# Last mixture-of-experts stage: one chain of gates, largest scores by comparison, experts of two blocks in one word, shared products earlier

## The reference, cut to what matters

```python
xt = layernorm(x).reshape(-1, 128)                       # 4096 tokens
scores = softmax(xt @ gate_w.T)                          # 4096 x 8
_, idx = top_k(scores + gate_bias, 2)
weights = take_along_axis(scores, idx, axis=1)
for e in range(8):
    gate_e = sum(where(idx == e, weights, 0), axis=1)
    h = silu(xt @ w1[e].T) * (xt @ w3[e].T)
    y = y + gate_e[:, None] * (h @ w2[e].T)
z = silu(xt @ sw1.T) * (xt @ sw3.T) @ sw2.T              # shared, 256 wide
x = x + y + z
```

## Time and profile before

| | |
|---|---|
| median of 3 runs | 1217.52 us (1216.44 to 1219.08) |
| the profiled execution, own time | 1217.4 us |
| its span | 1215.6 us |
| busy, share of the span | PE 79%, DVE 69%, ACT 53%, POOL 38% |
| granted clock of TensorE, mean | 0.898 of full |
| routing of the last stage | 980.7 to 1032.8 us |
| scatter | 1032.8 to 1082.7 us |
| expert blocks | 1082.7 to 1204.0 us |

### The profile page before, as it was taken

How to read it: one execution, slowest core, us unless ns; L and a number is a source line. 1 busy time by engine, 2 the same in 40 slices (tenths; PEclk the granted TensorE clock), 3 DMA queues, 4 the chain that set the end, 5 groups by cost and what they waited for, 6 DMA issues and landing times. The chain is left out here.

```text
span 1215.6 us, 21191 instructions
## 1 busy us (share of the span) xinstructions
PE 964.3 (79%) x7160; PEld 640.0 (53%) x7160; DVE 837.4 (69%) x2167; ACT 643.5 (53%) x1132; POOL 462.9 (38%) x448
## 2 busy tenths in 40 slices
PE   5868810578988997899669999998889886939995
PEld 3653310554556674454326666676645573627774
DVE  4586699857885664677679999999578856314332
ACT  3424568855643454565267877775466531114442
POOL 5610000002210003345099999994111230635443
PEclk9898965779999998999859999998899978969998
DMA  7000000064000000000000000000000000223331
GB/s 276 1 1 1 1 0 0 1 196 134 2 2 1 1 1 1 1 1 2 1 0 1 2 0 0 0 0 1 1 1 2 2 1 1 93 86 91 97 82 26
DMA packets 24235, 33.78 MB, mean 28 GB/s; under 512 B 3484, under 2 KB 20389, under 8 KB 23888
## 3 DMA queue, kind: packets, MB, share of 16 engines
q1 hardware_dynamic: 20720, 26.20, 7.1%
q0 software_dynamic: 3424, 6.38, 1.5%
HBM read 18.34 MB, written 15.98 MB: 28 GB/s over the span
## 5 line engine op out<-in xcount | busy, mean ns | idle before, releaser
L785 DVE TENSOR_REDUCE hq<-psum 128x16 f32<-128x1024 f32 x96 | 114.6, 1221 | 82.0 <-PE psum L519 44.2
L1975 POOL TENSOR_TENSOR big<-big 128x512 f32<-128x512 f32 x128 | 128.6, 1044 | 19.8 <-ACT big L1880 19.8
L429 POOL TENSOR_TENSOR big<-big,w_const 128x256 f32<-128x256 f32 x48 | 36.5, 762 | 260.1 <-PE psum L565 228.3
L1903 ACT ACTIVATE psum<-big,tmp 128x512 f32<-128x512 f32 x128 | 84.9, 686 | 18.9 <-DVE big L2072 16.2
L2580 DVE SCALAR_TENSOR_TENSOR big<-psum,big 128x128 f32<-128x128 f32 x118 | 36.1, 348 | 85.5 <-issue 65.7
L2072 DVE SCALAR_TENSOR_TENSOR big<-big,tmp,psum 128x512 f32<-128x512 f32 x128 | 90.5, 744 | 5.5 <-ACT psum L1903 2.5
L675 ACT ACTIVATE big<-psum 128x1024 f32<-128x1024 f32 x64 | 62.0, 1021 | 54.5 <-PE psum L549 54.5
L790 DVE RECIPROCAL big<-psum 128x256 f32<-128x256 f32 x48 | 84.0, 1751 | 6.1 <-PE psum L565 5.9
L2282 POOL DMA_INDIRECT out<-big x59 | 58.0, 982 | 69.5 <-DVE big L2590 36.9
L1985 POOL TENSOR_TENSOR big<-big 128x1024 f32<-128x1024 f32 x32 | 75.3, 2364 | 11.6 <-DVE big L2072 11.6
L1443 PE MATMUL psum<-f_downT,tmp 128*128 128x128 f32 x192 | 24.9, 293 | 68.0 <-DVE tmp L1326 68.0
(11 more groups left out here) (311 smaller groups left out, 2640.3 us busy)
## 6 DMA issues: line engine op xcount, KB each, us to landing
rows<-pad SPq DMA_DIRECT2D x1, 7670.0 KB, 34.1
big<-rows SPq DMA_DIRECT2D x59, 130.0 KB
tmp<-in_pack_f SPq DMA_DIRECT2D x1, 2051.0 KB, 9.7
w_f<-in_pack_f SPq DMA_DIRECT2D x1, 1280.0 KB, 12.5
tmp<-in_pack_once SPq DMA_DIRECT2D x1, 960.0 KB, 7.1
out<-big POOLq DMA_INDIRECT x59
X<-in_x SPq DMA_DIRECT2D x1, 768.0 KB, 5.2
w_a<-in_pack_a SPq DMA_DIRECT2D x3, 256.0 KB, 8.0
```

The lines of the kernel that those rows point to most:

```text
L785: dve.tensor_reduce(nm, psum[:, 1 + 2 * t:3 + 2 * t, :].rearrange("p c (r l k) -> p (c r) l k", r=2, k=SK), AX.X, ALU.max, negate=True).th ...
L1903: act.activation(bank(EX_BANK + h % 2), ssum[t][:, h * 512:(h + 1) * 512], ACT.Exp, bias=shift2[:, t * NH2 + h:t * NH2 + h + 1]).then_inc( ...
L1975: ins = pool.tensor_tensor(ssum[t][:, h * 512:(h + 1) * 512].rearrange("p (i j) -> p i j", i=ROWS2), st[:, 0, h, 0:ROWS2].unsqueeze(2).to_ ...
```

## The change

Parts of it, in the order of the kernel:
- Normalising: groups 1, 2, 7 on ACT, 3, 4, 5 on POOL. ACT takes group 1 before it finishes the second part of the LayerNorm.
- PE does up(0,0) before the turn of group 1 and up(0,1) after that of group 2. All logits go to one bank, and there is one chain of gates over 32 tiles, behind all logits.
- The two largest scores come by comparison: largest value, where it is equal, times 8 - expert, largest of that; the first is pushed down by 3e38 and the same is done again. MAX8 and FIND_INDEX8 go. The pair's number is worked out from the reversed indices, with constants to match.
- For groups 0 to 2 ACT also copies the second factor out of PSUM, and POOL multiplies; up(g, e) for g = 1 to 3 waits for ACT. DVE does groups 3 to 7.
- PE's order is up(1,0), up(1,1), down(0), up(2,0), up(2,1), counts, down(1), firsts, up(3,0), places, up(3,1), down(2), and on. `places` waits for oh3 and makes the table's products first, one instead of two; add(0) follows the gate columns on DVE.
- The table holds, for two blocks, four experts of five bits in one word. PE loads one word in every second turn, before the transpose, and works out each address with a shift and an AND.
- POOL has a drain ahead of the loop over the blocks and one in its middle.

```diff
@@ -2162,13 +2162,12 @@
+        up3 = [f3.take(GN) for _ in range(2)]
...
-        top3 = f3.take(N_TILES * 8).rearrange("p (t e) -> p t e", e=8)
-        ix3 = f3.take(N_TILES * 8).bitcast(U32).rearrange("p (t e) -> p t e", e=8)
-        ixf3 = f3.take(N_TILES * 2).rearrange("p (t e) -> p t e", e=2)
+        which3 = [f3.take(N_TILES) for _ in range(2)]
@@ -2192,8 +2192,14 @@
-        PARTS3 = ((0, EARLY), (EARLY, N_TILES))
-        ON_ACT, ON_POOL, ON_DVE = (1, 3, 7), (2, 4, 5), (0, 6)
+        POOLED = 3
+        SIL3 = 4 * POOLED + 2 * (N_GROUPS - POOLED)
...
+        def sil_count(g, e):
...
+            return 4 * g + 2 * e + 2 if g < POOLED else 2 * POOLED + 2 * g + e + 1
...
+        ON_ACT, ON_POOL, ON_DVE = (1, 2, 7), (3, 4, 5), (0, 6)
         def f3_normed(pe, g):
@@ -2234,12 +2240,9 @@
-            if 4 * g == EARLY:
-                pe.wait_ge(sem("a3", "res"), at("a3", "res") + N_GROUPS + 1)
-            part = int(4 * g >= EARLY)
...
-                c = 4 * g + t - PARTS3[part][0]
-                ins = pe.matmul(bank(5 + part)[:, c * E3:(c + 1) * E3], hT3[g][:, t * P:(t + 1) * P], W["f3_gate"],
+                c = 4 * g + t
+                ins = pe.matmul(bank(5)[:, c * E3:(c + 1) * E3], hT3[g][:, t * P:(t + 1) * P], W["f3_gate"],
@@ -2266,7 +2269,14 @@
-            pool.wait_ge(S("f3_m"), 6)
+            for g in range(POOLED):
+                for e in range(2):
+                    pool.wait_ge(S("f3_sil"), sil_count(g, e))
+                    if g >= 2:
+                        pool.wait_ge(S("f3_y"), g - 1)
+                    pool.tensor_tensor(hid3[2 * (g % 2) + e], sil3[e], up3[e], ALU.mult).then_inc(S("f3_hid"), 1)
...
+            pool.wait_ge(S("f3_m"), 5)
@@ -2275,7 +2285,10 @@
+            pool.drain()
             for j in range(NB3):
+                if j == NB3 // 2:
+                    pool.drain()
@@ -2297,7 +2310,9 @@
         def f3_pe(pe):
             def up(g, e):
...
-                if g:
+                if 0 < g <= POOLED:
+                    pe.wait_ge(S("f3_sil"), sil_count(g - 1, e))
+                elif g:
@@ -2316,20 +2331,21 @@
             def counts():
-                pe.wait_ge(S("f3_m"), 2)
+                pe.wait_ge(S("f3_m"), 1)
...
             def firsts():
-                pe.wait_ge(S("f3_m"), 3)
+                pe.wait_ge(S("f3_m"), 2)
...
             def places():
...
+                pe.matmul(bank(6)[0:1, 448:508], W["f3_lohi"][0:PAIRS3, :], oh3[0:PAIRS3, :], start=True, stop=True)
@@ -2337,40 +2353,55 @@
-                pe.wait_ge(S("f3_m"), 5)
-                for i in range(2):
-                    ins = pe.matmul(bank(5 + i)[0:1, 448:508], W["f3_lohi"][0:PAIRS3, i:i + 1], oh3[0:PAIRS3, :],
-                                    start=True, stop=True)
...
+            up(0, 0)
...
-            for g in range(2, N_GROUPS):
+            f3_turn(pe, 2)
+            pe.wait_ge(sem("a3", "res"), at("a3", "res") + N_GROUPS + 1)
+            up(0, 1)
+            f3_logits(pe, 1)
+            for g in range(3, N_GROUPS):
...
-            up(0, 0)
-            up(0, 1)
...
+            up(1, 1)
...
-            up(1, 1)
+            up(2, 0)
+            up(2, 1)
...
-            up(2, 0)
...
-            up(2, 1)
+            up(3, 0)
...
-            for g in range(3, N_GROUPS):
+            up(3, 1)
+            down(2)
+            for g in range(4, N_GROUPS):
...
-            pe.wait_ge(S("f3_m"), 7)
+            pe.wait_ge(S("f3_m"), 6)
...
-            first = {}
+            words = {}
...
+            def weights_at(j, k):
...
+                field = 2 * (j % 2) + k
+                w = words[j // 2]
+                w = w << 7 - 5 * field if field < 2 else w >> 5 * field - 7
+                return (w & 31 * P).with_bounds(min_val=0, max_val=(E3 - 1) * 3 * P)
...
             for i in range(NB3 + 3):
+                if i < NB3 and i % 2 == 0:
+                    m = i // 2
+                    _, (words[m],) = nc.values_load_multi_w_load_instructions(
+                        tab3[0:1, m:m + 1], engines=[mybir.EngineType.PE], min_val=0, max_val=2 ** 20 - 1,
+                        skip_runtime_bounds_check_because="the table holds experts' offsets alone")
@@ -2379,16 +2410,12 @@
-                    first[j] = [nc.values_load(tab3[0:1, 64 * k + j:64 * k + j + 1], engines=[mybir.EngineType.PE],
-                                               min_val=0, max_val=(E3 - 1) * 3 * P,
-                                               skip_runtime_bounds_check_because="the table holds experts' offsets alone")
-                                for k in range(2)]
...
-                    for k, r in enumerate(first[j]):
+                    for k in range(2):
...
-                                        W["f3_w"][:, ds(r, 2 * P)], start=True, stop=True)
+                                        W["f3_w"][:, ds(weights_at(j, k), 2 * P)], start=True, stop=True)
@@ -2404,33 +2431,30 @@
-                    for k, r in enumerate(first[j]):
+                    for k in range(2):
...
-                                        W["f3_w"][:, ds(r + 2 * P, P)], start=(k == 0), stop=(k == 1))
+                                        W["f3_w"][:, ds(weights_at(j, k) + 2 * P, P)], start=(k == 0), stop=(k == 1))
...
         def f3_act(act):
-            def exps(part):
-                lo, hi = PARTS3[part]
-                act.wait_ge(S("f3_less"), part + 1)
-                act.activation(prob3[:, lo:hi, :], prob3[:, lo:hi, :], ACT.Exp).then_inc(S("f3_ex"), 1)
...
             def silu(g, e):
...
-            f3_norm_act(act, 3)
+                if g < POOLED:
+                    act.wait_ge(S("f3_up"), 4 * g + 2 * e + 2)
+                    act.activation(up3[e], bank(4 + 3 * e), ACT.Copy).then_inc(S("f3_sil"), 1)
...
+            f3_norm_act(act, 2)
+            f3_take(act, 1)
...
-            f3_take(act, 1)
...
-            f3_take(act, 3)
...
-            for g in range(4, N_GROUPS):
+            for g in range(3, N_GROUPS):
...
-            exps(0)
-            exps(1)
+            act.wait_ge(S("f3_less"), 1)
+            act.activation(prob3, prob3, ACT.Exp).then_inc(S("f3_ex"), 1)
@@ -2459,51 +2483,53 @@
-            def gates(part):
...
-                lo, hi = PARTS3[part]
+            def gates():
...
+                lo, hi = 0, N_TILES
...
-                logits = bank(5 + part)[:, 0:n * E3].rearrange("p (t e) -> p t e", e=E3)
-                dve.wait_ge(S("f3_lg"), hi // GT)
+                logits = bank(5)[:, 0:n * E3].rearrange("p (t e) -> p t e", e=E3)
+                dve.wait_ge(S("f3_lg"), N_GROUPS)
...
-                dve.wait_ge(S("f3_ex"), part + 1)
+                dve.wait_ge(S("f3_ex"), 1)
...
-                settle(dve)
-                for t in range(lo, hi):
-                    dve.max(top3[:, t, :], bias3[:, t, :]).then_inc(S("f3_top"), 1)
-                dve.wait_ge(S("f3_top"), hi + lo)
-                for t in range(lo, hi):
-                    dve.max_index(ix3[:, t, :], top3[:, t, :], bias3[:, t, :]).then_inc(S("f3_top"), 1)
-                dve.wait_ge(S("f3_top"), 2 * hi)
-                step(dve.tensor_copy(ixf3[:, sl, :], ix3[:, sl, 0:2]))
-                step(dve.tensor_tensor(lo3[:, sl], ixf3[:, sl, 0], ixf3[:, sl, 1], ALU.min))
-                step(dve.tensor_tensor(hi3[:, sl], ixf3[:, sl, 0], ixf3[:, sl, 1], ALU.max))
-                step(dve.scalar_tensor_tensor(out=pid3[:, sl], in0=lo3[:, sl], scalar=-13.0, in1=lo3[:, sl],
-                                              op0=ALU.add, op1=ALU.mult))
-                step(dve.scalar_tensor_tensor(out=pid3[:, sl], in0=pid3[:, sl], scalar=-0.5, in1=hi3[:, sl],
-                                              op0=ALU.mult, op1=ALU.add))
+                rev = W["f3_exp"].unsqueeze(1).to_broadcast([P, n, E3])
...
+                def largest(which):
...
+                    step(dve.tensor_reduce(mx3, bias3, AX.X, ALU.max))
+                    step(dve.tensor_tensor(eq3[0], bias3, bc(mx3), ALU.is_equal))
+                    step(dve.tensor_tensor(eq3[0], eq3[0], rev, ALU.mult))
+                    step(dve.tensor_reduce(which, eq3[0], AX.X, ALU.max))
...
+                largest(which3[0])
+                step(dve.tensor_tensor(eq3[0], rev, bc(which3[0]), ALU.is_equal))
+                step(dve.scalar_tensor_tensor(out=bias3, in0=eq3[0], scalar=-3e38, in1=bias3, op0=ALU.mult, op1=ALU.add))
+                largest(which3[1])
+                step(dve.tensor_tensor(lo3, which3[0], which3[1], ALU.max))
+                step(dve.tensor_tensor(hi3, which3[0], which3[1], ALU.min))
+                step(dve.scalar_tensor_tensor(out=pid3, in0=lo3, scalar=-3.0, in1=lo3, op0=ALU.add, op1=ALU.mult))
+                step(dve.scalar_tensor_tensor(out=pid3, in0=pid3, scalar=-0.5, in1=hi3, op0=ALU.mult, op1=ALU.subtract))
...
-            def gate_columns():
+            def gate_column(i, a):
...
-                for i, a in enumerate((lo3, hi3)):
```

(50 more changed lines are left out.)

## The result

The changed kernel takes 1197.99 us (median of four runs, 1197.03 to 1200.55) against 1216.98 us for the kernel before (four runs): ratio 0.983, 95% interval 0.981 to 0.986. The profiled execution took 1197.03 us with a span of 1195.2, against 1215.6, so 20.4 us less. The forecast was 1202.1 us, between 1192 and 1212, with 0.93 for faster.

A forecast was written before the change was run, and what follows sets the result against it. Routing, scatter and expert blocks stand one behind the other, so each saving moves the end. -3.0 - 7.3 - 2.8 - 2.3 = -15.4 us from 1217.52 gives 1202.1 us, range 1192 to 1212.

The forecast's parts named there:

- Start of the gates: Up to the last logits: group 1 earlier and two shared products in PE's gap save 3.0 us (ends -6.3 and +0.5).
- I take the middle: End of the last logits: 996.5, between 993.2 at full clock and 1000 if the clock falls as before.
- The gate chain: From the last logits to the first scatter: 26.1 us instead of 33.4, so -7.3 us (ends -9 and -5.5).
- M is ready at L + 9.7: DVE's gate chain in routing: its result M stands 9.7 us after the last logits end, at 1006.2 instead of 1011.0.
- Scatter: The 32 scatters: PE's larger lead over POOL leaves one pause of 2.8 us less, -2.8 us (ends -5.7 and 0).
- Blocks: Expert blocks: 1.78 us a block instead of 1.87, 5.2 us in all, less grown stalls, net -2.3 us.
- a stall of 0.95 becomes 1.3, and comes every 7.4 blocks: Expert blocks: stalls read as instruction fetches grow with the shorter loop and more instructions, from 0.12 to 0.17 us a block.
- The drains: POOL's drains cost nothing, since POOL idles over half of a block; cover gone, 0 to 2 us once.
- 1: Expert blocks: shift and AND without reuse, 1.96 us a block, +4.7 instead of -2.3; 1209.1 us, chance 0.20.
- 3: Expert blocks: PE's sequencer becomes the bound; at 0.2 us an instruction 2.29 us a block, 1228.8 us; chance 0.05.
- 4: Routing and scatter: half clock as before, counts at 17 to 18 us after the logits, holds as before; 1212.5 us, chance 0.06.
- 2: Routing and scatter: the clock stays full and no hold is left, together -23.3; 1194.2 us, chance 0.12.

The follow-up runs named there:

- e11: The changed kernel with POOL's six products of groups 0 to 2 cut to one column of 512 (output wrong there); median 1196.1 us, ratio 0.982.
- e8: The changed kernel with up(0,0) and up(0,1) moved from amid the turns to behind the last logits; median 1198.6 us, ratio 0.984.
- e12: The changed kernel with the two largest scores found by MAX8 and FIND_INDEX8 again, in the one chain; median 1196.7 us, ratio 0.982.
- e9: The changed kernel with a memset of 128x512 on POOL ahead of scatter 8, 16 and 24; median 1198.2 us, ratio 0.983.
- e1 to e4: On one chip: changed kernel without its POOL drains, or with one every 8th block; kernel before with the drains, or shared words, alone; 1195.0, 1198.4, 1210.5, 1205.9 us.
- e7: The changed kernel with the drain behind the scatters alone, without the one among the expert blocks; median 1200.1 us, ratio 0.985.
- e2: The changed kernel with a POOL drain ahead of every 8th expert block instead of one in the middle; median 1198.4 us, ratio 0.989.
- e10: The changed kernel with a drain on POOL ahead of scatter 8, 16 and 24; median 1199.6 us, ratio 0.985.

## Why the prediction was right, and where it was not

**Start of the gates, -3.0: -2.7.** Right in size partly by luck. The attention stage ended 1.2 us later in this execution; from the last attention product the logits end 3.9 us sooner. "I take the middle" stood for a clock between full and half. What came was full clock from 986 to 996, but half clock under up(0,0), where the prediction looked for 1.00 up to 988. Where the clock never fell (e11) the logits end 12.7 us behind the last attention product instead of 18.8, -6.1, the -6.3 of the forecast's end. (Its own numbers for that end, half of the 15.1 us behind 984.35, give 991.9; where the other 1.3 us to its 993.2 come from it does not say.) e8 and the count of traces beside it bear out that the two products keep the clock up.

**The gate chain, -7.3: -5.6.** "M is ready at L + 9.7" is what e11 measures without POOL (9.8); with POOL it is 11.7, since DVE steps wait beside POOL's products, which the sum did not have. That "M is not the bound" was right, by 3.7 us, and e12 confirms it. Of the missing 1.7 us, 1.2 is PE's stretch up to the counts, 11.5 us instead of 10.3, most of it the clock: half for its first 5.3 us, which costs 2.6 where the sum allowed 1.7. The rest is the prefix sums, 1.75 instead of 1.05 us beside POOL's last product, less the little that was shorter than thought. What removed the wait of the earlier trace rows is the order together with POOL's multiplying, which no run parts, and not the new way to find the two largest.

**Scatter, -2.8: -1.8.** "One pause of 2.8 us less" failed: two holds stayed, of 1.0 and 2.9 us. The reading that POOL's issuing without pause holds the signal is too simple: pauses of 0.54 us do not end it (e9), and e1 to e4 issue in the same way on another chip and have no hold. That issuing every 1.26 us sets the rest was right: 39.5 us.

**Blocks, -2.3: -4.8.** The new loop was right (1.78 forecast, 1.79 found, reuse included). The old one was read from a single pair of blocks, 3.74 us; its median over the whole stretch is 3.83, so the loop gave 6.7 us and not 5.2, and the stalls of before were 4.6 us and not 0.12 a block, 7. What failed besides is "a stall of 0.95 becomes 1.3, and comes every 7.4 blocks", which adds 2.9: the stalls grew from 4.6 to 6.5 us, 2.9 of that at the drain, so the others shrank. Without the drain in the middle they are 1.35 us (e7) on the chip where the kernel before has 2.77. The fetches are still there in e7 (DMA view of 1074 to 1181), so the eight of them cost at most those 1.35 us:

```profile
q8 instruction: 8, 0.13, 0.5%
```

What stalls the kernel before no run shows. The rule of the Trainium skill that the prediction set against the trace (Runtime: NRT & Kernel Launch, Instruction fetch mechanics) would have given 1199.2, and was the better of the two: with eight fetches and 1.35 us of stalls in all in e7, the trace agrees that a crossing is mostly hidden.

**The drains, 0: -5.0 and +2.7.** The step that failed is "The drains on POOL cost nothing, as it idles over half of a block (cover gone: 0 to 2 us once)". It asked only what a drain costs. It did not look at the 10.2 us between the last output's issue and the end of the kernel before, 7.5 of which were the last drain of POOL's queue. The 2.7 us are the stall of the drain in the middle, inside the -4.8 of the blocks.

The rivals: 1 fell (no ALU instruction at the down products), 3 fell (1.79 a block), 4 fell. 2 was right on the clock of the turns, but not ahead of them, and wrong on the holds. The total missed by 4.1 us. That is luck in part: by the traces the end and the blocks gave 7.5 us more than forecast, and the gates, the scatter and the start 3 us less.

## What to carry to other kernels

Account for the whole span, up to the last row: a stretch of 10 us in which no engine computes is a term, and the queue rows of the engine that ends last show what it is. An operation that clears a queue is to be read from both sides, what it costs where it is put and what it takes off where the queue would have been cleared otherwise; here it was free in the traces where the queue's owner waits anyway, and no clear gain in the middle of a ring. When two engines are given work at the same time, ask whether both read SBUF with two operands. When a wait recurs, look at a second chip before an order of instructions is blamed for it.

## What was not expected of the hardware

- A drain on POOL behind indirect DMAs at the program's end takes about 0.082 us for each issue since the drain before it (7.50 for 91, 4.87 for 59, 2.50 for 30, 0.29 for 3), and ends 1.5 to 2.2 us behind the end of the last issue where it stands right behind eight (e2, e10).
- During a run of indirect DMAs on some chips DVE and ScalarE wait up to 12.8 us for signals from PE (e11), up to about 10 us beyond the end of the product that they wait for (in after ScalarE starts at 1047.27, the product ended at 1037.48): 10 traces, and none of 4 on another chip. Pauses of 2.6 us with a drain nearly end it, pauses of 0.54 us without one do not.
- DVE steps of 0.42 us took up to 1.37 beside a POOL product, and that product, 1.26 alone, up to 1.86 beside DVE (2.00 in e10).
